# A graph attention layer whose 0/1 matrix is turned partly by DVE in squares of 32, with its loads on two queues

## The chip, the cores and the metric

The kernel runs on one core of a Trainium2 chip. The metric is the device time of one execution in microseconds (us). The core has a matrix engine (PE), a vector engine (DVE), a scalar engine (ACT), GpSimd (POOL) and SyncE (SP), which here only issues DMAs. Each engine has its own instruction stream and runs it in order; they meet at semaphores.

## What is computed

```python
def layer(h, adj, W, a):                      # h, x: 4096 x 128; adj: 4096 x 4096 int32, 0 or 1
    Wh = h @ W
    a1, a2 = (a[:Fout, 0], a[Fout:, 0])
    e = (Wh @ a1)[:, None] + (Wh @ a2)[None, :]
    e = jnp.where(e > 0, e, 0.2 * e)
    e = jnp.where(adj > 0, e, -9e15)
    attention = jax.nn.softmax(e, axis=1)
    return jax.nn.elu(attention @ Wh)

h = jnp.maximum(_layernorm(x, axis=-1), 0.0)
x = x + layer(h, adj, W, a)
```

The matrix adj is 64 MB in HBM and has to be read once. About one entry in 512 is 1.

## The kernel before

The 4096 rows are cut in four chunks of 1024 rows (C = 4) and the 4096 columns in eight blocks of 512 (U = 8). A unit is one block of columns for one chunk of rows: 128 partitions with 8 rows each, 512 numbers a row, 2 MB. It is loaded as two halves of 1 MB by SP (`load_raw`, L249) into a ring of four slots, `raw`. All loads of adj are on SP's queue.

A unit goes through four engines. ACT makes bytes of 0 and 1 (`to_bytes`, L420), one instruction a half, into a ring of four slots, `mask`. PE turns it (`turn`, L817): 16 transposes of 128x128 byte pairs into PSUM, double-buffered as `mask_t`, so that columns of adj lie on partitions. DVE makes four words of it (`weights`, L610), one for each of the four columns q that a partition holds: 128x1024 four-byte elements, a maximum of two exponentials times the byte, kept as two fp16 halves. PE multiplies each word with the values (`product`, L834 to L836): 24 matmuls of 128x129, three for each of the eight tiles of rows, added up in `acc` in PSUM over all units of a chunk. `words` has four buffers, so DVE can be four words ahead of PE.

On PE the turn of unit u + 1 stands before the products of unit u in chunks 1 to 3. ACT may overwrite a slot of `mask` when PE has turned the unit four before. SP may overwrite a slot of `raw` when ACT has made bytes of the unit four before.

At the end of a chunk DVE takes the sums out of PSUM and the reciprocal of the normalizer (`take_sums`, L618 and L621), in the middle of the next chunk's unit 0. POOL, ACT and DVE make the output of it during that next chunk: POOL divides (L358) and takes the negative part (L362), ACT takes Relu and Exp (L483, L484), POOL adds x (L364), DVE adds the rest (`result`, L626), ACT stores (`store`, L488). In the last chunk a finer version of this runs after the last product and is stored by SP (L270 to L275).

Before all this, in chunk 0, a prologue normalizes x, projects it on PE, and makes the exponentials and the values (`val`, fp16, a high and a low part). POOL makes part of the values and then sums up `wh_sb` (L348 to L354). ACT squares the values for a check of their range (`square`, L432) between the bytes of the last unit of chunk 0 and those of chunk 1. If the check fails, a general path runs; it doesn't with these inputs.

## Time and profile before

| | |
|---|---|
| median of 3 runs | 245.03 us (244.39 to 245.18) |
| the profiled execution | 244.79 us |
| its span, first to last instruction | 243.0 us |
| busy: PE, DVE, ACT, POOL | 227.0, 196.4, 156.2, 59.1 us |
| mean granted clock of PE | 0.982 |
| moved by DMA | 71.9 MB |

The span is the time between the first and the last instruction; 1.8 us of the execution lie around it. A busy time counts an engine's instructions, whether or not something waited for them. The rows below come from one execution. In the timeline the columns are start, duration from the first start to the last end of the group, engine, line, operation, output and input, count, and in square brackets the idle time of the engine ahead of it with what ended it.

### The profile page before, as it was taken

Reading aid. Unit: us, or ns where it says so; the run is one execution under the profiler, and the core shown is the slowest. Engines: PE = TensorE matmul, PEld = TensorE weight load, DVE = VectorE, ACT = ScalarE, POOL = GpSimd, SP = SyncE. Lnnn points to the kernel's source line nnn. Section 1 sums busy time; section 2 is a strip of 40 time slices with the busy share of each in tenths; the row PEclk is TensorE's granted clock in tenths of the full one; section 3 lists DMA queues with packets and bytes.
Section 4 is the critical chain, followed back from the end, with each engine's and each line's share of the span. In section 5 each row is a group of like instructions: output and inputs, shape, how many; then the busy total and the mean of one; then the engine's idle time right before and its main releaser. Section 6 shows DMA issues by size and latency. Waiting matters only on the chain.

```text
span 243.0 us, 8254 instructions
## 1 busy us (share of the span) xinstructions
PE 227.0 (93%) x3736; PEld 221.2 (91%) x3736; DVE 196.4 (81%) x259; ACT 156.2 (64%) x139; POOL 59.1 (24%) x48
## 2 busy tenths in 40 slices
PE   6969999599999999999999999999999999999970
PEld 2759899599998999999999999999999999999970
DVE  4999997536776998889887988898879888998864
ACT  3698836697799999944996677019975774000051
POOL 3648036897000070300000560000001710040000
PEclk9997999999999999999999999999999999999995
DMA  6999999999998999999999999999999300020002
GB/s 225 360 389 386 386 386 385 388 367 370 301 352 284 363 395 386 388 385 385 398 386 385 388 385 385 385 387 369 386 386 386 140 0 3 3 89 3 3 0 92
DMA packets 36521, 71.92 MB, mean 296 GB/s; under 512 B 1282, under 2 KB 1924, under 8 KB 36484
## 3 DMA queue, kind: packets, MB, share of 16 engines
q1 hardware_dynamic: 35520, 69.74, 79.0%
q10 hardware_dynamic: 964, 1.64, 1.8%
q8 instruction: 30, 0.49, 0.8%
q14 instruction: 7, 0.06, 0.1%
HBM read 69.27 MB, written 2.10 MB: 294 GB/s over the span
## 4 chain that ended last, share of the span: by engine, by line
PE 74%; ACT 8%; DVE 7%; issue 4%; POOL 4%; DMA 1%; ACTq 0%; DVEq 0%; POOLq 0%
PE acc L834 20%; PE acc L835 20%; PE acc L836 20%; PE mask_t L817 11%; ACT mask L420 4%; POOL v L330 2%; POOL val L333 2%; ACT neg L432 1%; DVE words L610 1%; DVE stats L547 1%; DMA x_sb<-in_x_dram 1%; PE acc L796 1%; PE acc L805 1%; ACT neg L511 1%; DVE wh_sb L573 1%
## 5 line engine op out<-in xcount | busy, mean ns | idle before, releaser
L610 DVE SCALAR_TENSOR_TENSOR words<-g_row,gq_word,mask_t 128x1024 f32<-128x1024 f32 x128 | 161.4, 1278 | 36.0 <-PE acc L836 19.0
L834 PE MATMUL acc<-val,words 128*128 128x129 f16 x1000 | 171.9, 220 | 0.3 <-DVE wh_sb L573 0.3
L835 PE MATMUL acc<-val,words 128*128 128x129 f16 x1000 | 171.9, 220 | 0.0
L836 PE MATMUL acc<-val,words 128*128 128x129 f16 x1000 | 171.9, 220 | 0.0
L420 ACT ACTIVATE mask<-raw,step_bias 128x2048 uint8<-128x2048 int32 x63 | 121.8, 1993 | 28.4 <-DVE x_sb L626 17.3
L834 PEld LDWEIGHTS acc<-val,words 128*128 128x128 f16 x1000 | 97.8, 98 | 0.5 <-issue 0.5
L835 PEld LDWEIGHTS acc<-val,words 128*128 128x128 f16 x1000 | 97.9, 98 | 0.1
L836 PEld LDWEIGHTS acc<-val,words 128*128 128x128 f16 x1000 | 97.8, 98 | 0.0
L817 PE MATMUL mask_t<-ident_b,mask 128*128 128x128 bf16 x512 | 34.3, 221 | 1.8 <-ACT mask L420 1.8
L817 PEld LDWEIGHTS mask_t<-ident_b,mask 128*128 128x128 bf16 x512 | 30.3, 99 | 2.2 <-ACT mask L420 2.2
L358 POOL TENSOR_TENSOR hp<-num,rz 128x1024 f32<-128x1024 f32 x3 | 5.7, 1897 | 105.3 <-DVE rz L621 105.3
L508 ACT ACTIVATE v<-num,rz 128x128 f32<-128x128 f32 x6 | 2.0, 389 | 19.7 <-DVE rz L710 19.7
L412 ACT CAST val<-v 128x1024 f16<-128x1024 f32 (+1 forms) x5 | 4.4, 875 | 8.3 <-POOL v L330 8.3
L796 PE MATMUL acc<-w_sb,h_t 128*128 128x130 f32 x64 | 9.4, 305 | 0.3 <-ACT h_t L397 0.3
L796 PEld LDWEIGHTS acc<-w_sb,h_t 128*128 128x128 f32 x64 | 8.8, 217 | 0.7 <-ACT h_t L397 0.7
L364 POOL TENSOR_TENSOR hp<-hp,x_sb 128x1024 f32<-128x1024 f32 x3 | 7.1, 2375 | 9.3 <-ACT hp L483 9.3
L547 DVE BATCH_NORM_STATS2 stats<-x_sb 128x6 f32<-128x128 f32 x32 | 6.6, 275 | 2.7 <-DMA x_sb<-in_x_dram 2.7
L362 POOL TENSOR_SCALAR neg<-hp 128x1024 f32<-128x1024 f32 x3 | 8.3, 2776 | 0.5 <-POOL hp L358 0.5
L330 POOL TENSOR_TENSOR v<-wh_sb,dv 128x1024 f32<-128x1024 f32 x3 | 5.7, 1902 | 9.8 <-DVE val L588 9.8
L312 POOL TENSOR_TENSOR half_rstd<-var,minus_half 128x8 f32<-128x8 f32 (+1 forms) x5 | 7.0, 1394 | 4.2 <-DVE var L557 4.2
L860 PE MATMUL mask_t<-ident_b 128*128 128x512 bf16 x16 | 5.8, 502 | 2.2 <-POOL seed_row L306 2.2
L389 ACT ACTIVATE hn<-x_sb,twice 128x128 f32<-128x128 f32 x16 | 5.2, 392 | 3.6 <-DVE twice L553 3.6
(91 smaller groups left out, 125.4 us busy)
## 6 DMA issues: line engine op xcount, KB each, us to landing
raw<-in_adj_dram SPq DMA_DIRECT2D x64, 1024.0 KB, 14.1
x_sb<-in_x_dram SPq DMA_DIRECT2D x8, 256.0 KB, 5.7
out_dram<-x_sb ACTq DMA_DIRECT2D x3, 512.0 KB, 7.9
out_dram<-x_sb SPq DMA_DIRECT2D x2, 128.0 KB, 2.4
out_dram<-x_sb SPq DMA_DIRECT2D x1, 192.0 KB, 1.9
w_sb<-in_L_gnn_W_dram ACTq DMA_DIRECT2D x1, 64.0 KB
out_dram<-x_sb SPq DMA_DIRECT2D x1, 64.0 KB, 1.6
a_sb<-in_L_gnn_a_dram ACTq DMA_DIRECT2D x1, 1.0 KB
```

The source lines that it names most:

```text
L312: nc.gpsimd.tensor_tensor(half_rstd[:, t0:t1], var4[:, t0:t1], minus_half[:, 0:t1 - t0], ALU.pow).then_inc(rstd_ready, 1)
L330: nc.gpsimd.tensor_tensor(v32[:, g % 2], wh_sb[:, group(g), 0:F], dv[:, group(g)].unsqueeze(2).broadcast_to([P, CT, F]), ALU.mult).then_in ...
L362: nc.gpsimd.tensor_scalar(neg[:], hp[:], 0.0, None, ALU.min).then_inc(neg_ready, 1)
L364: nc.gpsimd.tensor_tensor(hp[:], hp[:], x_sb[:, group(c)], ALU.add).then_inc(sum_ready, 1)
L420: nc.scalar.activation(mask[:, u % RING, k * BT:(k + 1) * BT], raw[:, u % RING, k * BT:(k + 1) * BT], ACT.Sign, scale=1.0, bias=step_bias[ ...
L547: last = nc.vector.bn_stats(stats[:, t, :], x_sb[:, t, :])
L610: nc.vector.scalar_tensor_tensor(words[:, q], g_row[:, c * CHUNK:(c + 1) * CHUNK], gq_word[:, 1, t:t + 1], maskt_bytes[:, u % 2, q // 2, : ...
L796: last = nc.tensor.matmul(bank[:, t - t0], h_t[:, (2 * g + t // BT) % 4, (t % BT) * P:(t % BT + 1) * P], w_sb[:], start=True, stop=True)
L817: last = nc.tensor.transpose(maskt_pairs[:, u % 2, h, t * P:(t + 1) * P], mask_pairs[:, u % RING, t, :, h], ident_b[:])
L834: nc.tensor.matmul(acc_tile(t), high, val[:, tile, 0, 0:V], start=first and t % PT == 0, stop=False, skip_group_check=True)
L835: nc.tensor.matmul(acc_tile(t), high, val[:, tile, 1, 0:V], start=False, stop=False, skip_group_check=True)
L836: last = nc.tensor.matmul(acc_tile(t), low, val[:, tile, 0, 0:V], start=False, stop=False, skip_group_check=True)
```

## The change

Chunks 1 to 3 (`SETS` = 1, so every chunk from 1 on) treat units 4 to 7 together as a set. The set is loaded as four loads h = 0 to 3 of 2 MB. Load h brings, for a quarter of the chunk's rows, the columns of unit 4 to partitions 0 to 31, those of unit 5 to 32 to 63, of unit 6 to 64 to 95 and of unit 7 to 96 to 127, each by a DMA of 512 KB. SP issues the lower two and ACT the upper two. ACT makes bytes of each load in two instructions into three areas of 16 KB a partition (`pairs`), two of them over tensors that only chunk 0 uses, the third over slots 2 and 3 of `mask`. DVE turns a unit by one instruction in squares of 32x32 four-byte elements (`turn_set`), into the same PSUM buffers as before; it stands in DVE's stream before the last word of the unit ahead, and the first of a chunk waits for the bytes of all four loads. PE no longer turns these 12 units.

The columns then lie on other partitions, so POOL copies the second half of the values to match (`move_values`, 16 copies of 32 partitions) over x of chunks 2 and 3, once, after its sums of chunk 0. Each row's x is loaded again for chunks 1 to 3 (three DMAs of 512 KB on SP), since these chunks now have eight consecutive rows on a partition. From the 13th unit load on, ACT issues the second half of each ordinary unit too. The bytes of ordinary units of chunks 1 to 3 have two slots, not four. The order of units in chunks 2 and 3 is 0, 1, 4, 2, 5, 3, 6, 7. The squares move from the end of chunk 0 to behind the bytes of the 15th to 18th load. The output of a chunk is made by ACT (Relu of -h, Exp) and POOL (Relu less one, plus x, plus the exponential); DVE no longer takes part except in the last chunk. The last chunk is stored by three DMAs in place of four.

```diff
+    SETS = C - 3
+    ORDER = [[*range(U)] if c <= SETS else [0, 1, 4, 2, 5, 3, 6, 7] for c in range(C)]
+    SHARED = U + RING
+    LOADS = [(c, u, None) for c in range(SETS) for u in range(U)]
+    LOADS += [(SETS, u, None) for u in range(4)] + [(SETS, None, h) for h in range(4)]
+    for c in range(SETS + 1, C):
+        LOADS += [(c, 0, None), (c, None, 0), (c, None, 1), (c, 1, None), (c, None, 2), (c, None, 3), (c, 2, None), (c, 3, None)]
...
+    adj_set = adj.rearrange("(c h r t) (s k j) -> c s h k r t j", h=4, r=QUARTER, t=CT, k=4, j=BLOCK)
...
+        def turning(c, u):
+            if c < SETS:
+                return c * U + u + 1, c * U + u + 1 - RING
+            i = SETS * U + (c - SETS) * 4 + u
+            return i + 1, i + 1 - (RING if i < SETS * U + 2 else 2)
...
+            def load_set(at):
+                c, _, h = LOADS[at]
+                for k in SP_QUARTERS:
+                    sp.dma_start(raw[k * QUARTER:(k + 1) * QUARTER, at % RING], adj_set[c, 1, h, k]).then_inc(set_in[at % RING], 16)
...
+            for at in range(1, C * U):
+                if LOADS[at][1] is None:
+                    sp.wait_ge(act_bytes, 2 * (at - RING) + 1)
+                    load_set(at)
+                else:
+                    for k in range(2 if at < SHARED else 1):
...
+                        load_raw(at, k)
...
+            def move_values():
...
+                for k in range(4):
+                    for m in range(4):
+                        if moves:
+                            pool.wait_ge(val_moved, moves)
+                        moves += 1
+                        nc.gpsimd.tensor_copy(val_set_u[k * QUARTER:(k + 1) * QUARTER, 4 * m:4 * m + 4],
+                                              val_u[m * QUARTER:(m + 1) * QUARTER, (4 + k) * BT:(5 + k) * BT]).then_inc(val_moved, 1)
...
             def to_bytes(c, u, k):
...
+                if (c, u) >= (0, RING):
+                    act.wait_ge(turned, turning(c, u)[1])
...
+            def set_to_bytes(c, h):
+                at = LOADS.index((c, None, h))
+                act.wait_ge(set_in[at % RING], 64 * FILLED[at])
+                for k in range(2):
...
+                        act.wait_ge(set_turned, 4 * (c - SETS) + 2 * k - 4)
+                    nc.scalar.activation(pair_bytes[PAIRS[c][k]][:, :, h],
+                                         raw[:, at % RING, :, k * 256:(k + 1) * 256].rearrange("p t (m x) -> p m t x", m=2), ACT.Sign,
+                                         scale=1.0, bias=step_bias[:, 0:1]).then_inc(act_bytes, 1)
+            def load_half(at):
+                if SHARED <= at < C * U:
...
+            for at in range(U, C * U):
+                c, u, h = LOADS[at]
+                if u is None:
+                    set_to_bytes(c, h)
+                else:
                     for k in range(2):
                         to_bytes(c, u, k)
...
+                load_half(at + RING)
+                if at == 13:
+                    tail(0)
+                if 14 <= at < 14 + G:
+                    square(at - 14)
+                if at == 15:
+                    store(0)
...
+            def turn_set(c, i):
+                m = ORDER[c][i] - 4
+                if m == 0:
+                    dve.wait_ge(act_bytes, 2 * LOADS.index((c, None, 3)) + 1)
+                dve.wait_ge(words_ready, 4 * (c * U + i - 1))
+                nc.vector.transpose(maskt_quads[:, i % 2].rearrange("p (t h r) -> p t h r", h=4, r=QUARTER),
+                                    pair_quads[PAIRS[c][m // 2]][:, m % 2]).then_inc(set_turned, 1)
...
                 for u in range(U):
                     for q in range(BT):
+                        if q == BT - 1 and u < U - 1 and is_set(c, ORDER[c][u + 1]):
+                            turn_set(c, u + 1)
                         weights(c, u, q)
...
+            def turn_ahead(c, i):
+                if i == U - 1:
+                    c, i = c + 1, -1
+                if not is_set(c, ORDER[c][i + 1]):
+                    turn(c, i + 1)
```

## Rows read from the trace of the kernel before

**Rows 1.** The page, busy us, share of the span and instructions of each engine

```profile
PE 227.0 (93%) x3736; PEld 221.2 (91%) x3736; DVE 196.4 (81%) x259; ACT 156.2 (64%) x139; POOL 59.1 (24%) x48
```

**Rows 2.** The chain that ended last, in order of time: start us, us, what

```profile
84.22 0.89 PE mask_t L817 x16
90.55 0.89 PE mask_t L817 x16
...
223.55 0.89 PE mask_t L817 x16
```

**Rows 3.** Timeline of DVE from 60 us on

```profile
61.22 4.85 DVE L610 SCALAR_TENSOR_TENSOR words<-g_row,gq_word,mask_t 128x1024 f32<-128x1024 f32 x4 [2.35 <-PE mask_t L817]
...
84.09 1.35 DVE L618 TENSOR_TENSOR num<-acc,seed_row 128x387 f32<-128x387 f32 x3
85.48 0.20 DVE L621 RECIPROCAL rz<-num 128x8 f32<-128x8 f32 x1
...
92.91 5.29 DVE L610 SCALAR_TENSOR_TENSOR words<-g_row,gq_word,mask_t 128x1024 f32<-128x1024 f32 x4 [1.04 <-PE acc L836]
...
110.79 1.22 DVE L626 SCALAR_TENSOR_TENSOR x_sb<-neg,hp 128x1024 f32<-128x1024 f32 x1
```

**Rows 4.** Timeline of ACT from 60 us on

```profile
69.19 1.04 ACT L432 ACTIVATE neg<-val 128x1024 f32<-128x1024 f16 x1
70.14 0.19 ACT L432 ACTIVATION_READ_ACCUMULATOR neg<-val 128x1 f32 x1
70.36 1.06 ACT L432 ACTIVATE neg<-val 128x1024 f32<-128x1024 f16 x1
...
73.78 22.82 ACT L420 ACTIVATE mask<-raw,step_bias 128x2048 uint8<-128x2048 int32 x12
96.50 1.04 ACT L483 ACTIVATE hp<-hp 128x1024 f32<-128x1024 f32 x1
97.44 1.04 ACT L484 ACTIVATE neg<-neg 128x1024 f32<-128x1024 f32 x1
```

**Rows 5.** Windows: stretch, us, busy PE, PEld, DVE, ACT, POOL, clock, DMA share, GB/s

```profile
60.00:79.00 19.00, 18.57 (x322) 18.37 (x320) 13.87 (x13) 17.34 (x16) 0.00 (x0) 1.00 0.95 316
103.00:190.00 87.00, 87.00 (x1542) 87.00 (x1540) 74.47 (x66) 58.41 (x32) 9.72 (x5) 1.00 1.05 384
115.50:118.50 3.00, 3.00 (x57) 3.00 (x55) 1.88 (x3) 3.00 (x3) 0.00 (x0) 1.00 1.05 400
190.00:200.00 10.00, 10.00 (x181) 10.00 (x179) 8.24 (x7) 7.02 (x6) 4.37 (x2) 1.00 0.08 31
```

**Rows 6.** Groups by line and shape: busy us, mean ns of one, idle before

```profile
L610 DVE SCALAR_TENSOR_TENSOR words<-g_row,gq_word,mask_t 128x1024 f32<-128x1024 f32 x128 | 161.4, 1278 | 36.0 <-PE acc L836 19.0 <-PE mask_t L817 13.4
```

**Rows 7.** DMA issues: two of SP in its timeline, and ACT's by their line

```profile
90.94 0.54 SPq L249 DMA_DIRECT2D raw<-in_adj_dram  x1
...
92.83 2.83 SPq L249 DMA_DIRECT2D raw<-in_adj_dram  x1
...
L488 ACTq DMA_DIRECT2D out_dram<-x_sb x3: 379/395/424, 112.0 to 213.4; - x3
```

**Rows 8.** Windows, columns as in rows 5, around a gap of PE in the prologue

```profile
16.00:18.00 2.00, 0.27 (x2) 0.27 (x3) 1.97 (x6) 2.00 (x5) 2.00 (x4) 1.00 1.05 388
19.00:20.00 1.00, 1.00 (x15) 1.00 (x13) 1.00 (x7) 1.00 (x3) 0.69 (x1) 0.60 1.06 391
```

**Rows 9.** Timeline of POOL

```profile
56.66 2.64 POOL L354 TENSOR_TENSOR v<-v 128x512 f32<-128x512 f32 x3
85.83 1.90 POOL L358 TENSOR_TENSOR hp<-num,rz 128x1024 f32<-128x1024 f32 x1 [26.52 <-DVE rz L621]
...
138.56 2.77 POOL L362 TENSOR_SCALAR neg<-hp 128x1024 f32<-128x1024 f32 x1 [0.17 <-POOL hp L358]
```

**Rows 10.** Timeline of SP, its last two issues

```profile
239.50 0.58 SPq L273 DMA_DIRECT2D out_dram<-x_sb  x1
240.14 0.42 SPq L275 DMA_DIRECT2D out_dram<-x_sb  x1
```

More of the change, by code:

```diff
@@ L37 @@
 RING = 4
+QUARTER = 32
 WORDS = 4
@@ L48, in bass_graph_attention @@
     U = NB
+    SETS = C - 3
[5 more added lines that the diff above has]
+        LOADS += [(c, 0, None), (c, None, 0), (c, None, 1), (c, 1, None), (c, None, 2), (c, None, 3), (c, 2, None), (c, 3, None)]
+    FILLED = [len([b for b in range(a % RING, a + 1, RING) if (LOADS[b][1] is None) == (LOADS[a][1] is None)]) for a in range(C * U)]
     V = F + 1
@@ L155, in turned_bank, with rows_of, is_set, mask_slot @@
             return mask_t[:, 1, b % 2, :]
+        def rows_of(c):
+            if c < 2:
+                return x_sb[:, group(c)]
+            t0 = T * VP // 2 + (c - 2) * CHUNK
+            return val_f32[:, t0:t0 + CHUNK].rearrange("p (t f) -> p t f", f=F)
+        def is_set(c, u):
+            return c >= SETS and u >= 4
+        def turning(c, u):
[3 more added lines that the diff above has]
+            return i + 1, i + 1 - (RING if i < SETS * U + 2 else 2)
+        def mask_slot(c, u):
+            return u % RING if c < SETS else u % 2
         x_in = [sem(f"x_in{b}") for b in range(NB)]
@@ L159, in bass_graph_attention @@
         raw_in = [[sem(f"raw_in{s}_{k}") for k in range(2)] for s in range(RING)]
+        set_in = [sem(f"set_in{i}") for i in range(RING)]
+        set_turned = sem("set_turned")
+        pad_clear = sem("pad_clear")
+        pad_ready = sem("pad_ready")
+        val_moved = sem("val_moved")
+        rows_in = [sem(f"rows_in{c}") for c in range(C)]
         first_bytes = sem("first_bytes")
@@ L428, in square @@
             def square(g):
-                if g >= 1:
+                if g == 0:
+                    act.wait_ge(vh_ready, 2 + G - 1)
+                    act.wait_ge(ht_ps, NB)
+                else:
                     act.wait_ge(squares_ready, g)
-                nc.scalar.activation(neg[:], val[:, group(g), 0, 0:F], ACT.Square, accum_out=squares[:, g:g + 1]
+                nc.scalar.activation(squared, val[:, group(g), 0, 0:F], ACT.Square, accum_out=squares[:, g:g + 1]
                                      ).then_inc(squares_ready, 1)
@@ L816, in turn, with value_tile, product @@
                     for t in range(CT):
-                        last = nc.tensor.transpose(maskt_pairs[:, u % 2, h, t * P:(t + 1) * P], mask_pairs[:, u % RING, t, :, h], ident_b[:])
+                        last = nc.tensor.transpose(maskt_pairs[:, i % 2, h, t * P:(t + 1) * P],
+                                                   mask_pairs[:, mask_slot(c, u), t, :, h], ident_b[:])
                 last.then_inc(turned, 1)
-            def product(c, u, q):
-                n = c * U + u
-                first = (u, q) == (0, 0)
+            def value_tile(c, i, q):
+                u = ORDER[c][i]
+                return val_set[:, (u - 4) * BT + q] if is_set(c, u) else val[:, u * BT + q]
+            def product(c, i, q):
+                n = c * U + i
+                first = (i, q) == (0, 0)
                 pe.wait_ge(words_ready, 4 * n + q + 1)
-                tile = u * BT + q
+                if is_set(c, ORDER[c][i]):
+                    pe.wait_ge(val_moved, MOVES)
+                v = value_tile(c, i, q)
                 for t in range(CT):
@@ L906, in _ @@
                 if u == U - 1:
-                    turn(0, u + 1)
+                    turn_ahead(0, u)
                 for q in range(BT):
@@ L930, in _ @@
                     else:
-                        turn(c, u + 1)
+                        turn_ahead(c, u)
                         for q in range(BT):
```

210 lines of the change are left out of this document (133 added, 77 removed).

## Prediction

> **What bounds the kernel now.** I read the page's busy shares first [rows 1]: PE is busy for 93% of the span, DVE for 81%, ACT for 64%. Shares are averages, so the chain of work that ended last comes next [rows 2]. From 77.7 us on it holds nothing but PE: a turn of one unit (16 transposes, 0.89 us) every 6.33 us, from 84.22 (the turn of unit 1 of chunk 1) to 223.55 (unit 7 of chunk 3). So a unit costs 0.89 of turning and 5.44 of products. I number units through the kernel: 8 to 15 are chunk 1, 16 to 23 chunk 2, 24 to 31 chunk 3. Products of unit 8 begin at 84.22 + 0.89 = 85.1.
>
> How near are the others? DVE makes a unit's four words in 4.85 us where nothing holds it [rows 3], so one word costs (4.85 - 1.28)/3 = 1.19 and a unit 4.8; in the steady state the four take 5.29 and 1.04 of idle, waiting for PE [rows 3]. ACT turns a unit to bytes in two halves at 22.82/12 = 1.90 each [rows 4]. The DMA moves 384 GB/s from 103 to 190 us and is nearly idle afterwards [rows 5]: 2.1 MB of a unit take 5.46, less than PE's 6.33. In short, per unit: PE 6.33, DMA 5.46, DVE 4.8, ACT 3.8. A gain on PE is soon limited by the next two.
>
> **The transposes leave PE.** In chunks 1 to 3 the units 4 to 7 are no longer turned on PE: 12 times 0.89 = 10.7 us less on the path. If nothing else came late, that would be the gain.
>
> **DVE takes them.** Twelve 32x32 turns of 128x1024 four-byte elements, SBUF to PSUM. No row shows one. Nearest are DVE's other 128x1024 instructions: 1.22 for the one that read two SBUF tensors [rows 3], 1.28 for a word [rows 6]. I take 1.2. Below, 0.6 would be two elements for each step, for which no row of DVE over 1024 elements speaks; above I allow 2.3, twice the work. It loses three results, 1.22 each, to POOL. A chunk is then 32 x 1.19 + 4 x 1.2 + 1.55 of sums [rows 3] = 44.5 on DVE, against 8 x 5.44 + 4 x 0.89 = 47.1 on PE. On average PE still bounds, but not in a run of set units (units 4 to 7): 4 x 1.19 + 1.2 = 6.0 on DVE against 5.44 on PE.
>
> **The wait that it adds, and this is the term I think decides.** The first turn of a chunk waits for the bytes of all four set loads (each holds a quarter of the rows of units 4 to 7). It stands in DVE's queue ahead of the last word of the unit before, so PE's last product of that unit waits too. In chunk 1 the order is 0 to 7, so this is at unit 11. When are the bytes there? Only two slots are left for the bytes of units turned on PE, so ACT's bytes of unit 11 wait for PE's turn of unit 9, done at 85.1. ACT runs in order from there: unit 11, 3.8 us; its half of a set load, two DMAs. Nearest rows: 0.395 for a 512 KB issue on ACT, 0.54 for 1 MB on SP where the queue isn't full [rows 7]; I take 0.45 each, 0.9 a set and 0.55 an ordinary half. Then set load 0, 3.8, issue 0.55; set load 1, 3.8, issue 0.9; tail of chunk 0 (Relu and Exp at about 1.0 each [rows 4] and a handshake), 2.05; set load 2, 3.8, issue 0.9; one square, 1.2 [rows 4]; set load 3, 3.8. The sum from 85.1 is 4.7 + 4.35 + 4.7 + 2.05 + 5.9 + 3.8 = 25.5: 110.6. The turn makes it 111.8, the word 113.0. PE would have wanted it after units 8, 9, 10, two turns and three of four tiles of unit 11: 85.1 + 16.3 + 1.8 + 4.1 = 107.3. So PE stalls for 5.7.
>
> After that DVE has no lead, and units 12 to 14 go at 6.0, not 5.44, with some start-up: 1.8 more. From unit 16 on PE bounds again. In chunk 2 set units alternate with others. From 110.6 on ACT has six units of 3.8, issues of 4.0, three squares and a store, 4.0, ahead of the last set bytes of that chunk: 141.4, against 146 wanted (unit 16 starts at 139.8, and the fourth tile of unit 17 is due at 149, a turn and a word behind the bytes). In chunk 3 the load decides: it is third from the end of a stream that ends at 192 (below), so it lands at about 182 and is in bytes by 187, against 192 wanted. No stall in either, with some 5 us to spare.
>
> PE's clock could fall in the stall. A gap of PE (0.27 busy in 2 us) was followed within 3 us by a granted clock of 0.60 on the mean of a microsecond [rows 8], so part of it ran at 1.2 in place of 2.4 GHz. Here the products behind the stall wait for DVE anyway and DVE's words go on; I take nothing and keep 2 us for the range.
>
> **POOL.** Its sums end at 59.3; its next work is at 85.8 [rows 9]. Sixteen copies of 32x640 elements go between, one waiting for the other. A 128x1024 instruction takes 1.90 to 2.77 there [rows 9], 1.9 to 2.7 ns an element, so 1.2 to 1.75 a copy, 19 to 28 in all: done by 88 at the latest. The tail of chunk 0 behind it is wanted by ACT at about 98.9. Hidden, and it would stay so up to some 2.4 a copy. POOL also takes over the third addition of a tail: ACT's store of chunk 0 comes at 112, POOL is through at about 107. Hidden.
>
> **Small ones.** The squares leave the place where they delayed the bytes of unit 8 [rows 4], but DVE's words bound there at once, so 0.1. A DVE copy in the prologue, 0.2 longer. At the end three stores, not four: the last issue starts some 0.6 earlier [rows 10].
>
> **DMA.** 1.5 MB of x are loaded again, 4.1 us at 384 GB/s. The dip at 60 to 79 us (316 GB/s [rows 5]) partly closes, since ACT frees slots sooner. The last load lands near 192 as now. An ordinary half is issued in 0.54 on SP where few are queued and 2.83 where more are [rows 7]; each queue now holds half as many, so I take 0.54 on ACT.
>
> **Sum.** -10.7 + 5.7 + 1.8 - 0.1 + 0.2 - 0.6 = -3.7, rounded to -3.5 for the handshakes that I left out. The profiled execution took 244.79 (span 243.0), 0.24 below the median of 245.03. So 241.3 for such an execution, **241.5** beside the median. Its own range is 238.5 to 244.2: set DMAs and byte instructions may cost ACT up to 10% more or less, a turn 1.0 to 1.6 (each 0.1 us is worth 0.4 in units 12 to 15), the clock up to 2.
>
> **Rivals.** (1) *Set loads are slower* (ends slower than before). A set load is four DMAs of 32 partitions each, SP the lower 64 partitions and ACT the upper. For it: no row shows a load that writes fewer than 128 partitions. Against: when ACT's store and SP's loads ran together the total was 400 GB/s [rows 5], so two queues share the DMA engines without loss, and as SP and ACT are released by the same bytes they would run side by side. Price: 12 set loads of 2.1 MB each; at r GB/s each costs 2097/r - 5.46 more, less some 5 us of slack. At 310 GB/s it is 16 - 5 = 11: 252.5. At 192, half of today's rate, as if only one queue's half of the partitions were served at a time, it is 65 - 5 = 60: 302. It costs the whole gain below 341 GB/s. Chance that it is below that: 0.18.
> The Trainium skill speaks for this rival. "SBUF — State Buffer", section "Door 1: The DMA port swizzle", gives 189 GB/s for partitions 0 to 31 and 196 for 0 to 63, and the section "Can I just issue two DMAs to hit both halves?" says that they serialize, only 6% faster than one; by that the time would be near the 302. The trace's 400 GB/s had all 128 partitions on both queues, so it doesn't settle this.
> (2) *DVE becomes the bound.* At 2.3 a turn a set unit takes 7.1 on DVE and a chunk 49.0 against 47.1: 3.3 more in chunk 1, some 2 in each of the others: 249. For it: nothing but the lack of a row. 0.07.
> (3) *ACT is later still:* set issues at 0.9 a DMA, or byte instructions with the scattered output at 2.2. Each takes 3 to 4 us more into the stall: 245.3, no change. 0.13.
> (4) *POOL's copies take 3 us each:* they end at 107, ACT waits for the tail, the stall grows by 10: 252. 0.05.
> (5) *The stall isn't there*, since PE reaches unit 11 later or ACT earlier than computed: 235.8. 0.07.
> Forecast: 0.50.
>
> **Range and chances.** 236 to 254 leaves out the lower part of (5), 0.04, and the worse part of (1), 0.13. A measurement here tells 0.3%, 0.7 us, from no change. Faster: 0.50 + 0.07 + 0.02 of (3) = 0.59; within: 0.10 of (3); slower: 0.18 + 0.07 + 0.05 + 0.01 = 0.31.
>
> **What would show it.** In the trace after: no transposes on PE for set units, and a unit of 5.44 there. A DVE turn of 1.2. One PE gap near 107 to 113, ended by a word that waited for ACT's bytes, none like it in chunks 2 and 3. DMA at 380 GB/s or more while set loads run. POOL's copies over before 92. A DMA rate under 340 in the set loads, a gap before every chunk's first turn, or words on DVE back to back through all of chunks 2 and 3 would make it wrong.

## The result, and the profile after

The changed kernel takes 258.55 us (254.67 to 261.37, 4 runs); the kernel before takes 244.96 beside it (244.39 to 245.18, 4 runs). The ratio is 1.0465, with a 95% interval of 1.0351 to 1.0578. Ratios go by the means of the executions within 1.5% of the fastest of their kernel: for the changed kernel these are 254.67 and 257.82, with a mean of 256.2, and the cost of the narrow loads is worked out from such means below. The forecast was 241.5 with a range of 236 to 254: wrong in sign and outside the range. The profiled execution took 257.82, with a span of 256.0.

Two rows of the page first, busy time by engine and the DMA rate in 40 slices of 6.4 us.

```profile
PE 222.8 (87%) x3544; PEld 215.7 (84%) x3544; DVE 202.1 (79%) x270; ACT 157.8 (62%) x139; POOL 80.9 (32%) x68
...
GB/s 220 370 387 386 387 383 386 387 387 389 363 356 279 342 363 340 331 317 340 339 357 318 286 384 330 290 330 300 293 289 324 303 366 82 0 84 3 3 4 83
```

PE has 192 matmuls less than in [rows 1], but its share of the span fell from 93% to 87%: it waits. The rate is near 387 up to the tenth slice and falls to 279 in the thirteenth, where the first set loads begin; it never comes back to stay. The windows say it by stage (columns as in [rows 5]).

```profile
60.00:79.00 19.00, 19.00 (x334) 18.98 (x332) 14.01 (x13) 15.26 (x9) 10.59 (x15) 1.00 1.04 351
79.00:103.00 24.00, 24.00 (x428) 24.00 (x426) 20.96 (x20) 17.13 (x10) 2.32 (x2) 1.00 1.06 339
103.00:130.00 27.00, 17.13 (x270) 16.95 (x268) 16.05 (x14) 21.68 (x18) 7.91 (x3) 0.81 1.06 329
130.00:160.00 30.00, 27.12 (x477) 26.78 (x475) 26.07 (x26) 19.16 (x12) 1.92 (x2) 1.00 1.06 338
160.00:190.00 30.00, 28.91 (x506) 28.49 (x504) 27.58 (x23) 16.45 (x9) 8.35 (x3) 1.00 1.05 296
190.00:215.00 25.00, 19.96 (x309) 19.62 (x307) 17.46 (x17) 16.71 (x9) 1.90 (x1) 0.88 0.92 304
```

Before, 384 GB/s ran from 103 to 190 us and the stream was over by 192 [rows 5]. Now it is at 339, 329, 338 and 296, and still at 304 from 190 to 215. The share of time in which the DMA engines are busy (next to last column) did not fall with the bytes: 1.06. They are not short of work; each packet takes longer. The chain of work that ended last shows what that costs. Before, it held nothing but PE from 77.7 us to the last turn [rows 2]; now three flights of set loads issued by ACT stand in it (start us, us, what), and loads of adj are 26.5% of the whole chain.

```profile
126.54 21.25 DMA raw<-in_adj_dram
...
152.36 20.58 DMA raw<-in_adj_dram
...
177.52 26.07 DMA raw<-in_adj_dram
```

PE lost its time in a few places. What PE waited for from 78 to 240 us, in all, how often, and the longest:

```profile
PE acc L1019 <- DVE words L796: 14.3, 3, 9.9
PE mask_t L995 <- ACT mask L535: 3.5, 2, 2.0
PE mask_t L995 <- issue: 0.9, 1, 0.9
```

The 9.9 stands at 106.6 to 116.4 (the end of the word in the row at 115.12 below), in chunk 1, where the prediction had its one stall of 5.7. DVE's and POOL's timelines show the two operations that no row of before had:

```profile
59.10 12.35 POOL L477 COPY first<-val 32x640 uint32<-32x640 uint32 x16
...
113.95 1.26 DVE L776 STREAM_TRANSPOSE mask_t<-second 128x1024 uint32<-128x1024 uint32 x1 [11.53 <-ACT second L553]
115.12 1.24 DVE L796 SCALAR_TENSOR_TENSOR words<-g_row,gq_word,mask_t 128x1024 f32<-128x1024 f32 x1
```

DVE waited 11.5 us for ACT's bytes (`second` is the area of the set bytes), turned in 1.26, made the word, and PE went on. ACT's own timeline up to that point:

```profile
85.88 3.90 ACT L535 ACTIVATE mask<-raw,step_bias 128x2048 uint8<-128x2048 int32 x2 [1.63 <-issue]
89.81 1.48 ACTq L564 DMA_DIRECT2D raw<-in_adj_dram  x2
91.42 3.90 ACT L553 ACTIVATE second<-raw,step_bias 128x2048 uint8<-128x2048 int32 x2 [1.64 <-issue]
95.35 0.49 ACTq L566 DMA_DIRECT2D raw<-in_adj_dram  x1
95.96 3.90 ACT L553 ACTIVATE second<-raw,step_bias 128x2048 uint8<-128x2048 int32 x2 [0.64 <-ACT second L553]
99.89 1.50 ACTq L564 DMA_DIRECT2D raw<-in_adj_dram  x2
101.43 1.06 ACT L632 ACTIVATE neg<-hp 128x1024 f32<-128x1024 f32 x1 [1.57 <-issue]
102.52 1.06 ACT L634 ACTIVATE neg<-neg 128x1024 f32<-128x1024 f32 x1
103.48 3.88 ACT L553 ACTIVATE second<-raw,step_bias 128x2048 uint8<-128x2048 int32 x2
107.40 1.48 ACTq L564 DMA_DIRECT2D raw<-in_adj_dram  x2
108.99 1.06 ACT L585 ACTIVATE first<-val 128x1024 bf16<-128x1024 f16 x1 [1.62 <-issue]
...
110.04 3.88 ACT L553 ACTIVATE second<-raw,step_bias 128x2048 uint8<-128x2048 int32 x2
```

It is the chain of the prediction in its order, and nothing in it waits for PE or for a load: every idle piece is an issue. In chunk 3 it is different:

```profile
176.90 2.92 ACTq L564 DMA_DIRECT2D raw<-in_adj_dram  x2
181.63 2.00 ACT L553 ACTIVATE second<-raw,step_bias 128x2048 uint8<-128x2048 int32 x1 [4.77 <-DMA raw<-in_adj_dram]
...
186.07 6.22 ACTq L642 DMA_DIRECT2D out_dram<-first  x1
192.40 3.90 ACT L535 ACTIVATE mask<-raw,step_bias 128x2048 uint8<-128x2048 int32 x2 [6.86 <-issue]
```

There ACT waits for loads (4.77), and the issue of a store, 0.4 before [rows 7], takes 6.22; the bytes of unit 25 stand behind it. With the wide loads tried below the same store takes 2.29 to issue. That it waits for room in ACT's queue is likely, but no run tried it.

### The profile page after: what moved, and what is told of

Read it like the earlier page. It is cut to its first block, busy times and chain, and to the rows that moved or that the text cites. A ratio compares the mean times of both kernels' runs of the same rounds, so it can differ in the third digit from the quotient of the medians.

```text
span 256.0 us, 7960 instructions
## 1 busy us (share of the span) xinstructions
PE 222.8 (87%) x3544; PEld 215.7 (84%) x3544; DVE 202.1 (79%) x270; ACT 157.8 (62%) x139; POOL 80.9 (32%) x68
## 2 busy tenths in 40 slices
DMA packets 36935, 73.47 MB, mean 287 GB/s; under 512 B 1698, under 2 KB 2212, under 8 KB 36900
## 4 chain that ended last, share of the span: by engine, by line
DMA 27%; PE 23%; ACT 21%; issue 10%; DVE 9%; ACTq 5%; POOL 4%; POOLq 0%; DVEq 0%
DMA raw<-in_adj_dram 27%; ACT mask L535 8%; ACT second L553 7%; DVE words L796 6%; ACTq L564 5%; PE acc L1019 4%; PE acc L1021 4%; PE acc L1020 4%; ACT mask L553 3%; PE mask_t L995 3%; PE mask_t L1052 2%; POOL second L421 2%; POOL val L424 2%; PE mask_t L963 2%; PE acc L974 1%
## 5 line engine op out<-in xcount | busy, mean ns | idle before, releaser
L1019 PE MATMUL acc<-val,words 128*128 128x129 f16 x640 | 112.4, 222 | 14.7 <-DVE words L796 14.3
L796 DVE SCALAR_TENSOR_TENSOR words<-g_row,gq_word,mask_t 128x1024 f32<-128x1024 f32 x80 | 99.4, 1273 | 25.5 <-PE mask_t L995 13.3
L1021 PE MATMUL acc<-val,words 128*128 128x129 f16 x640 | 112.5, 222 | 0.0
L1020 PE MATMUL acc<-val,words 128*128 128x129 f16 x640 | 112.5, 222 | 0.0
L535 ACT ACTIVATE mask<-raw,step_bias 128x2048 uint8<-128x2048 int32 x39 | 76.3, 1996 | 17.2 <-issue 11.7
L1019 PEld LDWEIGHTS acc<-val,words 128*128 128x128 f16 x640 | 63.4, 99 | 15.7 <-DVE words L796 14.8
L1020 PEld LDWEIGHTS acc<-val,words 128*128 128x128 f16 x640 | 63.4, 99 | 0.1
L1021 PEld LDWEIGHTS acc<-val,words 128*128 128x128 f16 x640 | 63.5, 99 | 0.0
L1019 PE MATMUL acc<-first,words 128*128 128x129 f16 x360 | 63.0, 223 | 0.0
L1020 PE MATMUL acc<-first,words 128*128 128x129 f16 x360 | 62.9, 222 | 0.0
L1021 PE MATMUL acc<-first,words 128*128 128x129 f16 x360 | 62.8, 222 | 0.0
L796 DVE SCALAR_TENSOR_TENSOR words<-g_row,first,mask_t 128x1024 f32<-128x1024 f32 x48 | 58.0, 1269 | 0.0
L553 ACT ACTIVATE second<-raw,step_bias 128x2048 uint8<-128x2048 int32 x16 | 31.5, 1993 | 14.3 <-DMA raw<-in_adj_dram 11.5
L1019 PEld LDWEIGHTS acc<-first,words 128*128 128x128 f16 x360 | 35.8, 99 | 0.0
L1020 PEld LDWEIGHTS acc<-first,words 128*128 128x128 f16 x360 | 35.8, 99 | 0.0
L1021 PEld LDWEIGHTS acc<-first,words 128*128 128x128 f16 x360 | 35.7, 99 | 0.0
L995 PE MATMUL mask_t<-ident_b,mask 128*128 128x128 bf16 x320 | 23.0, 229 | 5.7 <-ACT mask L535 4.9
L454 POOL TENSOR_SCALAR hp<-hp 128x1024 f32<-128x1024 f32 x3 | 10.9, 3633 | 50.5 <-ACT neg L632 50.5
L776 DVE STREAM_TRANSPOSE mask_t<-second 128x1024 uint32<-128x1024 uint32 x8 | 10.0, 1254 | 16.3 <-ACT second L553 11.5
L553 ACT ACTIVATE mask<-raw,step_bias 128x2048 uint8<-128x2048 int32 x8 | 15.9, 1991 | 7.0 <-DMA raw<-in_adj_dram 7.0
## 6 DMA issues: line engine op xcount, KB each, us to landing
first<-in_x_dram SPq DMA_DIRECT2D x8, 256.0 KB, 6.1
val<-in_x_dram SPq DMA_DIRECT2D x2, 512.0 KB, 20.7
```

The source lines that it names most:

```text
L454: nc.gpsimd.tensor_scalar(hp[:], hp[:], 0.0, -1.0, ALU.max, ALU.add).then_inc(pos_ready, 1)
L535: nc.scalar.activation(mask[:, mask_slot(c, u), k * BT:(k + 1) * BT], raw[:, at % RING, k * BT:(k + 1) * BT], ACT.Sign, scale=1.0, bias=st ...
L553: nc.scalar.activation(pair_bytes[PAIRS[c][k]][:, :, h], raw[:, at % RING, :, k * 256:(k + 1) * 256].rearrange("p t (m x) -> p m t x", m=2 ...
L776: nc.vector.transpose(maskt_quads[:, i % 2].rearrange("p (t h r) -> p t h r", h=4, r=QUARTER), pair_quads[PAIRS[c][m // 2]][:, m % 2]).the ...
L796: nc.vector.scalar_tensor_tensor(words[:, q], g_row[:, c * CHUNK:(c + 1) * CHUNK], word, bytes_t, ALU.max, ALU.mult).then_inc(words_ready, 1)
L995: last = nc.tensor.transpose(maskt_pairs[:, i % 2, h, t * P:(t + 1) * P], mask_pairs[:, mask_slot(c, u), t, :, h], ident_b[:])
```

## The experiments

All times below are medians beside a kernel before that took 244.6 to 244.9. Theory A: a DMA that writes 32 partitions gets less of the way into SBUF, and the two queues make up for it only in part. Its rivals: two queues disturb each other; the order in which a set load reads DRAM; ACT's chain; DVE.

### Which part of the loads is slow

**Two queues, ordinary loads.** The kernel before, with ACT issuing every second half from unit 12 on:

```diff
-                for k in range(2):
+                for k in range(2 if n < U + RING else 1):
...
+            def load_half(n):
+                if U + RING <= n < C * U:
+                    act.wait_ge(act_bytes, 2 * (n - RING) + 1)
+                    act.dma_start(raw[:, n % RING, BT:CT], adj_v[n // U, 1, n % U]).then_inc(raw_in[n % RING][1], 16)
```

> The kernel before with one part of the change alone: from unit 12 on ACT issues the second half of each unit, all loads still 128 partitions wide. Theory A (the loss of DMA rate belongs to the DMAs of 32 partitions): DMA stays at 384 GB/s from 103 to 190 us, 245 us, within 0.5 of before. Theory B (two queues that load at once lose rate by themselves): the rate falls towards the 320 to 340 GB/s of the changed kernel; the last load lands 15 or more us later and, as before had about 13 us of lead, the time rises by 2 to 6.

Measured: 244.5 us, ratio 1.0007 (0.998 to 1.0033). From 103 to 130 us:

```profile
103.00:130.00 27.00, 27.00 (x481) 27.00 (x479) 22.95 (x19) 22.92 (x13) 1.70 (x1) 1.00 1.05 389
```

389 GB/s on two queues, and no change in the time, as theory A expected. The second queue and ACT's issues cost nothing where ACT has time to spare.

**One queue, narrow loads.** The changed kernel with every load on SP:

```diff
-        SP_QUARTERS, ACT_QUARTERS = (0, 1), (2, 3)
+        SP_QUARTERS, ACT_QUARTERS = (0, 1, 2, 3), ()
```

> The changed kernel with every load issued by SP, the four quarters of a set load one after the other on one queue; ACT issues none. Theory A (32 partitions reach only part of the SBUF side, and only side by side do the lower and upper 64 partitions add up): set loads run near 200 GB/s, the last load lands after 260 us and the time is 290 or more. Theory B (two queues are the trouble): the rate returns to 384 and the time falls to 245 or less. Theory C (ACT's own time for issuing decides, not the rate): ACT is freed of 1.5 us a set load, the time falls by 3 or more.

Measured: 296.5 us, ratio 1.2151 (1.2074 to 1.2228).

```profile
79.00:103.00 24.00, 21.25 (x370) 20.83 (x368) 19.49 (x19) 15.59 (x9) 1.90 (x1) 1.00 1.07 218
```

218 GB/s while set loads run one after another, against 339 on two queues. So the two queues do add up, but not to twice.

**Wide loads.** As many DMAs with as many bytes, each two rows of all 128 partitions:

```diff
-                    sp.dma_start(raw[k * QUARTER:(k + 1) * QUARTER, at % RING], adj_set[c, 1, h, k]).then_inc(set_in[at % RING], 16)
+                    sp.dma_start(raw[:, at % RING, 2 * k:2 * k + 2], adj_lin[c, 4 + h][:, 2 * k:2 * k + 2]).then_inc(set_in[at % RING], 16)
```

and the same for ACT. These loads bring other entries than the layer needs for units 4 to 7, so this kernel measures the loads and can't be used. Bytes and packets are as in the changed kernel (73.47 MB in 36935 packets).

> The changed kernel with set loads of the same bytes and the same number of DMAs (two on SP, two on ACT), but each DMA 128 partitions by 2 rows in place of 32 partitions by 8 rows. The set bytes are then those of other elements, so units 4 to 7 of chunks 1 to 3 are computed from wrongly placed entries. Theory A: DMA at 380 GB/s or more throughout, last load near 195, only the stall ahead of the first set of chunk 1 stays (8 to 10 us); time 243 to 247. Theory B: the rate stays at 320 to 340 and the time at 255 or more.

Measured: 242.16 us (241.98 to 242.46), ratio 0.9899 (0.9883 to 0.9916). Its windows and PE's largest wait:

```profile
79.00:103.00 24.00, 24.00 (x428) 24.00 (x426) 20.68 (x20) 19.41 (x11) 4.59 (x2) 1.00 1.05 387
103.00:130.00 27.00, 19.62 (x306) 19.45 (x304) 18.82 (x16) 22.49 (x19) 5.66 (x3) 0.81 1.05 389
```

```profile
PE acc L1019 <- DVE words L796: 7.4, 1, 7.4
```

The rate is back and the stalls of chunks 2 and 3 are gone. Gap and time came out a little below the 8 to 10 and 243 to 247 expected, and the time is 0.7 above the forecast. The narrow loads cost 256.25 - 242.19 = 14.1 us (16.4 between the medians).

**Who takes which quarter.** SP takes quarters 0 and 2, ACT 1 and 3, so that both begin in the lower 64 partitions and go on to the upper together:

```diff
-        SP_QUARTERS, ACT_QUARTERS = (0, 1), (2, 3)
+        SP_QUARTERS, ACT_QUARTERS = (0, 2), (1, 3)
```

> The changed kernel with SP loading quarters 0 and 2 and ACT 1 and 3, so that both queues write first to the lower and then to the upper 64 partitions. Theory A with a bound by the half of the partitions: both queues go to the same half at once, the rate in set loads falls towards 200 GB/s, time 280 or more. If which half doesn't matter, only the width of a DMA: the time stays within 3 us of the changed kernel.

Measured: 287.7 us (283.6 to 291.8), as expected of a bound by the half.

```profile
79.00:103.00 24.00, 21.39 (x373) 20.97 (x371) 19.32 (x19) 14.60 (x9) 1.90 (x1) 1.00 1.07 222
...
160.00:190.00 30.00, 21.87 (x353) 21.31 (x351) 19.38 (x17) 21.59 (x12) 8.38 (x3) 0.89 1.06 312
```

With both queues in the same 64 partitions, two queues give 222 GB/s, as one did (218). From 160 us on, with ordinary loads in between, it is 312, against 289 with everything on SP; there the two queues may have drifted into different halves, but no row shows it. What is shared is the half of the partitions, not the queue.

**Destination or source.** Narrow places, but the rows of an ordinary unit:

```diff
-                    sp.dma_start(raw[k * QUARTER:(k + 1) * QUARTER, at % RING], adj_set[c, 1, h, k]).then_inc(set_in[at % RING], 16)
+                    sp.dma_start(raw[k * QUARTER:(k + 1) * QUARTER, at % RING], adj_lin[c, 4 + h][k * QUARTER:(k + 1) * QUARTER]).then_inc(set_in[at % RING], 16)
```

> The changed kernel with one edit: the 32-partition DMAs of a set load write the same places as before, but read the rows of an ordinary unit (a quarter of its partitions, 8 rows of 512 elements each from next to each other in DRAM) in place of the rows that belong there. So the entries of units 4 to 7 in chunks 1 to 3 are not those of the reference; bytes, DMAs, partitions and order are unchanged. Theory A (the narrow destination is what lowers the rate, since a DMA that writes 32 partitions uses only part of the way into SBUF): nothing changes; 325 to 345 GB/s from 79 to 160 us, last load near 215, time 255 to 262. Rival B (the order in which a set load reads DRAM lowers the rate, since that pattern gathers its rows from four places of a row of adj): 380 GB/s or more, last load near 193, time 241.5 to 243 as with the wide set loads.

Measured: 258.3 us (254.6 to 262.5), like the changed kernel.

```profile
79.00:103.00 24.00, 24.00 (x428) 24.00 (x426) 20.68 (x20) 17.39 (x10) 2.58 (x2) 1.00 1.06 346
```

Only the destination is as before the edit, and the loss is all there. These DMAs bring the same rows as the wide ones did, so between the two kernels only the partitions that one DMA writes differ. The reading order of DRAM is cleared. (This kernel, too, computes from other entries.)

### What the first stall is made of

**Four slots in chunk 1.** The prediction let ACT's bytes of unit 11 wait for PE's turn of unit 9, since two slots are left. Here they have four:

```diff
-            return i + 1, i + 1 - (RING if i < SETS * U + 2 else 2)
+            return i + 1, i + 1 - (RING if i < SETS * U + 4 else 2)
...
-            return u % RING if c < SETS else u % 2
+            return u % RING if c <= SETS else u % 2
...
-                        act.wait_ge(turned, SETS * U)
+                        act.wait_ge(turned, SETS * U + 4)
```

> The changed kernel with one edit: in chunk 1 the bytes of units turned on PE keep all four slots, and the second pair of set bytes waits for those units' turns in place of that. So ACT's bytes of unit 11 no longer wait for PE's turn of unit 9, and everything of ACT up to the last set bytes of chunk 1 moves ahead by up to the 5.7 us which that wait and the unit behind it cost. Theory A (the set loads' rate sets the end, the stall of chunk 1 is ACT's chain): the gap of PE at 106.6 shrinks from 9.9 to 4 to 5.5, since ACT then waits for the last set load of the chunk, which lands at 104.6; the later gaps grow because the loads are as slow as before: the last load still lands at 209 to 214, the time is 253 to 257. Rival (the first stall is paid in full on top of the slow loads): the whole 5 us is seen in the time, 252.5 to 254. Rival (the stall of chunk 1 isn't made by ACT's wait for a slot): the gap stays at 9 to 10 and the time at 258.

Measured: 256.4 us, ratio 1.0452 (1.0427 to 1.0478), where the changed kernel has 1.0465. ACT ahead of unit 11's bytes, and DVE's turn:

```profile
86.33 3.90 ACT L535 ACTIVATE mask<-raw,step_bias 128x2048 uint8<-128x2048 int32 x2 [1.62 <-issue]
```

```profile
114.40 1.26 DVE L776 STREAM_TRANSPOSE mask_t<-second 128x1024 uint32<-128x1024 uint32 x1 [11.73 <-ACT second L553]
```

The mechanism that was expected missed: the gap stayed at 10.1, as its second rival had it. The time lies in the 253 to 257 that were expected, but that is no credit to it, since the changed kernel's 256.2 lies there too. ACT came from an issue, not from a wait, so there was nothing to free. The slot wait of the prediction ended at 85.1, and ACT was not ready before 85.9 anyway.

**ACT without issues.** The wide loads, all on SP (the edits of the kernels with one queue and with wide loads together, so again with other entries):

> The kernel with wide set loads (same bytes and number of DMAs, each 2 rows of all 128 partitions, so that the entries of units 4 to 7 in chunks 1 to 3 are not those of the reference), with every load issued by SP. It measures what ACT's issues cost the chain to the last set bytes of chunk 1. Theory A (that chain is what PE waits for, and the issues are part of it): 3 x 1.1 + 0.6 = 3.9 us of issues leave it behind unit 11, so the gap of PE that was 7.4 with wide loads on two queues is 3.5 to 5; the rate stays at 380 or more; 238 to 240. Rival (one queue with 36 DMAs of 512 KB is slower than two): a rate below 370 and 242 or more.

Measured: 237.18 us (237.02 to 237.36), ratio 0.9687 (0.9668 to 0.9706). PE's wait in all, and ACT ahead of unit 11:

```profile
PE acc L1019 <- DVE words L796: 3.4, 4, 2.5
```

```profile
84.62 3.90 ACT L535 ACTIVATE mask<-raw,step_bias 128x2048 uint8<-128x2048 int32 x2 [2.44 <-PE mask_t L995]
```

The gap went from 7.4 to 2.5 and the time down by 242.16 - 237.18 = 5.0, both a little more than the 3.9 expected of the issues. One queue of SP carries wide loads at 388 GB/s from 103 to 130 us. And now ACT does wait for PE's turn, 2.44 us.

**The same with four slots:**

> The same with the bytes of chunk 1's units in four slots. Theory A: now that ACT has idle ahead of unit 11 (it waits for PE's turn of unit 9), the slot is worth something: the gap shrinks to 1 to 4, 236.5 to 239. Rival (ACT has no idle there even without issues): no change against the kernel with two slots.

Measured: 234.84 us (234.52 to 235.35), ratio 0.9601 (0.9581 to 0.9621).

```profile
PE acc L1019 <- DVE words L796: 0.8, 3, 0.3
```

The same edit that moved nothing above gives 2.3 us here. Gap and time are below the 1 to 4 and 236.5 to 239 expected. The stall is gone, and the kernel is 9.8 us faster than before (244.68 beside it); the prediction had 9.2 for the case without a stall. It still brings other entries: 234.84 says what the change is worth with loads at full rate, and is not a time of this layer.

### Wide loads that compute the same

The wide loads above bring other entries. To place the right ones with 128 partitions, a set load was cut by row, eight DMAs of one row each, all on SP:

```diff
-                for k in SP_QUARTERS:
-                    sp.dma_start(raw[k * QUARTER:(k + 1) * QUARTER, at % RING], adj_set[c, 1, h, k]).then_inc(set_in[at % RING], 16)
+                for t in range(8):
+                    sp.dma_start(raw[:, at % RING, t], adj_set[c, 1, h][:, :, t]).then_inc(set_in[at % RING], 16)
```

> The changed kernel computing the same, with two edits: a set load is cut by row (8 DMAs, each one row of all 128 partitions, 262 KB) instead of by partition (4 DMAs of 32 partitions), and SP issues every load, so ACT issues none. Theory A (the 32-partition DMAs were the whole loss): the rate is back at 380 to 390 GB/s although one queue carries all, the last adj load lands near 193; ACT's chain to the last set bytes of chunk 1 loses its issues (the 3 x 1.6 and 0.6 after unit 11), so the first gap of PE is 4 to 5 in place of 9.9; time 237.5 to 240. Rival (the rate needs two queues when loads are cut this way, or small DMAs are dear in themselves): a rate below 350 GB/s, a time over 245.

> The same with the bytes of chunk 1's units in four slots, as tried before with the narrow loads, where it moved nothing because ACT had no idle to give back. Theory A: with ACT's issues gone ACT reaches unit 11's bytes before PE's turn of unit 9, so now the slot does hold it, and freeing it shortens the first gap further, to 1 to 4; time 236.5 to 239. Rival (what is left of the gap is ACT's own byte work): the gap and the time stay as in the kernel with two slots.

> The changed kernel computing the same, with one edit: a set load is 8 DMAs of one row of all 128 partitions, four issued by SP and four by ACT, in place of 4 DMAs of 32 partitions. Theory A: 380 GB/s or more in the set loads, last adj load near 193; ACT's four issues cost 4 x 0.5 = 2.0 a set load (0.99 for two wide ones, as measured), so the first gap is 8 to 10 as before, and the time is 242.5 to 245. Rival (cutting by row gathers 2 KB pieces from all over a chunk and is as slow as the narrow DMAs): 325 to 345 GB/s, 255 or more.

Measured: 431.2, 431.6 and 429.6 us, ratios 1.761, 1.764 and 1.752. All three expectations missed by far: the rivals of the first and the third name the side, but nothing like the size. The windows of the first, while set loads run:

```profile
79.00:103.00 24.00, 24.00 (x428) 24.00 (x426) 20.67 (x20) 10.53 (x6) 1.90 (x1) 1.00 0.27 104
103.00:130.00 27.00, 3.26 (x58) 3.08 (x55) 0.00 (x0) 5.89 (x4) 6.97 (x3) 0.63 0.26 102
```

The DMA share fell to 0.26, a quarter of the usual 1.05, and the rate to 104 GB/s, a quarter of it too. Here the DMA engines are short of work: on average a quarter of them moves data. With ACT issuing half of the DMAs it was the same (0.27 and 103 GB/s), so it is not the queue. The source of such a DMA has four parts as its slowest dimension (the four quarters), then 32 rows. The Trainium skill, "DMA: Bandwidth & Descriptors", section "Why a DMA increments its semaphore by 16 and not by 1", says that a DMA is divided over the largest number of engines, up to 16, that divides the slowest dimension of both sides, and that on these queues they are always the first ones: by that four here, and the same four for every DMA. The trace agrees in the share, 0.26 of all engines, where four of sixteen kept at the usual 1.05 would give 0.26. No run tried another number of parts.

### Fewer sets

**Sets in the last chunk alone,** in the narrow form, with four slots; ACT issues halves from the first set load on:

```diff
-    SETS = C - 3
+    SETS = 3
...
-    SHARED = U + RING
+    SHARED = SETS * U + RING
```

> The changed kernel with sets in the last chunk alone (4 set loads in place of 12), its bytes in four slots as before the change, and the rows of x of chunks 2 and 3 loaded again. Theory A: the transposes of 4 units leave PE, 4 x 0.89 = 3.6 us; one store fewer gives 0.6; four set loads at 339 GB/s in place of 384 cost the stream 4 x (6.19 - 5.46) = 2.9 us, but the last adj load then lands at 196, before PE needs it; ACT is ahead of PE by then and no gap of PE over 2 us is left. 240.5 to 242.5, faster than the kernel before by 1 to 1.7%. Rival (DVE's turns and the sets' byte order cost more than PE's transposes even without the slow loads, so the gain is lost in gaps ahead of the last chunk's first turn): 244 to 247.

**Sets in chunks 2 and 3** (`SETS = 2`):

> As the kernel with sets in the last chunk alone, but with sets in chunks 2 and 3 (8 set loads). Theory A: 8 x 0.89 = 7.1 us leave PE, 0.6 of a store; the stream loses 8 x 0.73 = 5.8 and ends near 199 to 200. Chunk 2 runs its units in order 0 to 7, so its first turn needs all four set loads of the chunk; these land by about 152 and are in bytes by 155, where PE would want them at about 154: a gap of 0 to 4. Time 238 to 242.5. Rival (the slow loads cost nearly as much as in three chunks): 246 to 250.

Measured: 242.87 us, ratio 0.9916 (0.9885 to 0.9948), and 267.8, ratio 1.0893 (1.0858 to 1.0927). The first is just over its 240.5 to 242.5, the second misses its 238 to 242.5 by 25 us and is slower than sets in three chunks. Its first set loads from 115 to 130 us, SP's issues, and ACT:

```profile
115.00:130.00 15.00, 15.00 (x269) 15.00 (x267) 11.31 (x10) 5.71 (x5) 0.00 (x0) 1.00 1.06 277
```

```profile
114.58 27.84 SPq L323 DMA_DIRECT2D raw<-in_adj_dram  x8
```

```profile
107.87 2.27 ACTq L568 DMA_DIRECT2D raw<-in_adj_dram  x2
...
120.68 2.01 ACT L539 ACTIVATE mask<-raw,step_bias 128x2048 uint8<-128x2048 int32 x1 [2.61 <-DMA raw<-in_adj_dram]
128.06 2.00 ACT L539 ACTIVATE mask<-raw,step_bias 128x2048 uint8<-128x2048 int32 x1 [5.38 <-DMA raw<-in_adj_dram]
```

(Its profiled execution took 272.2.) ACT issued its half of the first set load at 107.9, when five halves of ordinary loads, 1 MB each, were still on the way in SP's queue (halves, not whole loads, as the expectation below puts it); SP issued its own at 114.6, behind four. So ACT's upper half flew beside ordinary loads, and SP's lower half later by itself.

**In step.** Both kernels with one edit, ACT issuing second halves from unit 12 on as in the changed kernel, so that SP's queue is no longer than ACT's when the sets begin:

```diff
-    SHARED = SETS * U + RING
+    SHARED = U + RING
```

> The kernel with sets in chunks 2 and 3, which took 267.8, with one edit: ACT issues the second half of every load from unit 12 on, as in the changed kernel, and not from the first set load on. It computes the same as the reference. In the slow one SP's queue held five whole ordinary loads when ACT issued its first half of a set load: ACT's half landed at 122, SP's at 144, so the two halves of the partitions were written one after the other. Theory A (lower and upper partitions add up only while both queues are at set loads together): 325 to 345 GB/s in the set loads in place of 277, chunk 2's first turn 0 to 3 us late in place of 13, time 239 to 244. Rival (set loads from chunk 2 on are slow for another reason): 260 or more.

> The kernel with sets in the last chunk alone, which took 242.9, with the same edit (second halves on ACT from unit 12 on). Theory A: the rate in its set loads, 290 GB/s in the first 15 us, becomes 330 or more, the gap of PE of 1.7 at 200 us goes, time 240.5 to 242.5. Rival (nothing depended on that): 242.9 as before.

Measured, two chunks: 254.6 us (248.5 to 258.0), ratio 1.0228 (1.0165 to 1.0292).

```profile
115.00:130.00 15.00, 15.00 (x269) 15.00 (x267) 12.23 (x11) 9.92 (x9) 0.00 (x0) 1.00 1.06 333
130.00:160.00 30.00, 28.63 (x507) 28.45 (x503) 20.90 (x20) 19.66 (x12) 4.90 (x2) 1.00 1.06 309
160.00:190.00 30.00, 25.49 (x415) 25.32 (x416) 27.87 (x24) 13.57 (x7) 5.33 (x3) 0.89 1.06 284
```

The first window rose from 277 to 333 GB/s, as expected, and the time fell by 13 us between the medians, but not to the 239 to 244 expected: from 130 us on the rate falls again, as it did in the changed kernel from 160 on (296). (The windows are of an execution of 256.0.) Why is not settled. The two queues may get out of step again where set and ordinary loads alternate. ACT's set DMAs take longer to land than SP's here (median 20.7 against 16.2 us), but so they do in the kernel with wide loads (11.0 against 8.6), so that doesn't show it.

Measured, last chunk alone: 241.63 us (241.13 to 241.98), ratio 0.9869 (0.9849 to 0.9889). The two stretches of its set loads:

```profile
160.00:175.00 15.00, 15.00 (x269) 15.00 (x267) 11.54 (x10) 9.23 (x5) 0.00 (x0) 1.00 1.06 315
175.00:190.00 15.00, 15.00 (x269) 15.00 (x267) 13.64 (x14) 10.14 (x6) 1.90 (x1) 1.00 1.06 365
```

Against 290 and 357 out of step, and the 1.7 us gap of PE is gone. The 315 is below the 330 that was expected; the time is within its 240.5 to 242.5. The medians differ by 1.2 us and the intervals just touch, so this step alone is hardly clear of the noise. This version computes the same as the kernel before and takes 1.3% less. Its slow loads stand at the end of the stream, where by the prediction's times some slack is left before PE needs them; no row here separates that from their smaller number.

## Why the prediction was wrong, step by step

**The sum held where its rate held.** With wide loads on two queues, 242.16 us against 241.5. That is nearer than the terms deserve: the stall was 7.4, not 5.7, and the rest together came out about 0.7 better than priced. With ACT relieved as well and four slots, 234.84 against 235.8 of rival (5), which was the case without the stall. So the terms for PE (-10.7), for DVE's pace, the store and the small ones are right together to within 1 us. DVE's pace in a run of set units was 5.9 from turn to turn (119.85, 125.75 and 131.64 in its timeline), against 6.0.

**DVE's turn.** Priced at 1.2, measured at 1.254. Right; rival (2) falls (its sum of 49.0 a chunk should read 48.8, which changes nothing).

**POOL's copies.** Priced at 1.2 to 1.75 each and over at 88; measured at 12.35/16 = 0.77, over at 71.5. Too dear, hidden either way; rival (4) falls.

**The stall in chunk 1.** It was seen in its place, but at 5.7 instead of 9.9. The last bytes came at 113.95, not at 110.6, and PE was there at 106.6, not 107.3: 3.35 + 0.75 = 4.1, nearly all of the 4.2 missing. The mis-sized term is ACT's issue of half a set load, taken at 0.9. In the timeline the idle for it is 1.6: three of them and one ordinary half are 1.64 + 0.64 + 1.57 + 1.62 = 5.5, not 3.25. An instruction to bytes pair took 3.90, not 3.8: 0.5 over five. And ACT came to unit 11 0.8 late, out of the issue before it, not out of the slot wait. So rival (3) was partly true. With wide loads an issue of two cost 1.12 of ACT's idle, and the gap was 7.4.

**The clock.** Taken as nothing, and that was right for this stall: the wide kernel's granted clock is 0.81 from 103 to 130 us, with a gap of 7.4, and the one with a gap of 2.5 stays at 1.00 there; between them the time differs by 5.0 and the gaps by 4.9. Nothing is left for the clock. After the stall DVE's words set the pace, and PE keeps up with them at the lower clock too: it is busy for all of the 14 us from 116 to 130, against 13.45 in the other kernel.

**The rate of the set loads, which is the step that failed.** The prediction took the set loads at 384 GB/s, because two queues had shown 400 together [rows 5], and gave slower set loads 0.18. The 400 was of loads and stores over all partitions; it said nothing on narrow ones, as the prediction itself noted. Measured: 339 from 79 to 103 us, just below the 341 from which its rival (1) decides. That rival had the mechanism and the sign, but its price was too low. At 339 its formula gives 12 x (2097/339 - 5.46) - 5 = 3.7, and the loads cost 14.1. That is nearly all of the miss: the change was forecast at -3.5 and measured at 256.2 - 244.9 = +11.4, which is 14.9 apart. What the formula left out: half of the loads from chunk 1 on are ordinary ones, so 339 in set loads and 384 in the others would give 2/(1/339 + 1/384) = 360 GB/s over a chunk, but the windows have 338 and 296 from 130 to 190. So either the ordinary loads are slowed beside narrow ones, or the set loads run below 339 once the queues are out of step, as the 277 above; no run separates the two. And ACT's waits for loads and its long issues stand in front of other work of ACT, as the 4.77 and the 6.22 above show. In the profiled executions, 257.82 and 242.46, the gaps of PE from 78 us to the end differ by 19.3 - 7.8 = 11.5 us. PE's busy time after the first 60 us differs by another 3.9 (170.2 against 166.3), part of it at the lower clock after the gap of 3.1 at 207 us (granted clock 0.77 from 205 to 220). Together that is the whole 15.4.

Loads into one half of the partitions alone ran at 218 GB/s on one queue and 222 on two in the same half. The Trainium skill, "SBUF — State Buffer", section "Door 1: The DMA port swizzle", gives about 218 GB/s as the ceiling for partitions 0 to 31 or 0 to 63. The trace agrees. The Trainium skill, "SBUF — State Buffer", section "Can I just issue two DMAs to hit both halves?", says that they serialize, at 6% above one. Here they reached 339, over 50% more than the 218, with deep queues of 512 KB DMAs, so the measurement differs, and the 302 us that stood beside that sentence were too pessimistic. The first section was right on which loads are slow, and rival (1) deserved more than the 0.18.

**Chunks 2 and 3 without a stall.** Wrong in the changed kernel, 9.0 us of gaps (the 19.3 less the 9.9 of chunk 1 and 0.4 at the end), and right with wide loads, none: this step fell only with the rate.

## What to carry to other kernels

A load that is cut by partition is a new kind of load: price it by the half of the partitions it writes (218 GB/s here for either half alone), and don't let a rate seen over 128 partitions stand for it. Cutting by row instead keeps the partitions but can leave the slowest dimension of the source at four, and here such loads kept a quarter of the DMA engines busy (share 0.26) and ran at 102 to 104 GB/s. Issues that an engine makes stand in its own chain: here 4.9 of 7.4 us of a stall were ACT's, and freeing a buffer was worth nothing until they were gone.

## What the runs showed of the hardware that was not expected

- Two queues writing to different halves add up in part: 333 to 339 GB/s where both began their set loads together (315 in the last chunk), 277 when SP's queue was behind, 222 in the same half. The DMA share is 1.06 or 1.07 in all of them, so a busy share near 1 says nothing on the rate.
- Issuing a DMA of 32 partitions costs ACT 0.57 us, and 0.89 for the next right behind it; two of 128 partitions with the same bytes take 0.99 together. From 169 us on, two of the narrow ones take 2.9, and a store 6.2.
- A DMA whose source has four parts as its slowest dimension ran at 102 to 104 GB/s with a share of 0.26, on one queue and on two.
- A 128x1024 turn in squares of 32, four-byte elements, takes 1.254 us into PSUM, like DVE's other passes over that many elements (1.22 and 1.28 in [rows 3] and [rows 6]).
